# Order of gathered sums and dense multiplications on TensorE in a four-layer graph network

## What is computed

```python
h = jnp.maximum(_layernorm(x, axis=-1), 0.0)
neigh = jax.ops.segment_sum(h[src], dst, num_segments=N_NODES)
x = x + (jnp.maximum(((1.0 + eps[0]) * h + neigh) @ W1 + b1, 0.0) @ W2 + b2)
h = jnp.maximum(_layernorm(x, axis=-1), 0.0)
agg = jax.ops.segment_sum(h[src], dst, num_segments=N_NODES)
x = x + jax.nn.relu(agg / jnp.maximum(cnt, 1.0)[:, None] @ W_l.T + b_l + h @ W_r.T)
```

## Time and profile before

| | us |
|---|---|
| median of 3 runs (lowest, highest) | 6944.7 (6934.82, 6959.4) |
| profiled execution, its own time | 6939.28 |
| its span | 6937.5 |
| dense turns of layer 2 in the trace, about | 5258 to 5943 |
| dense turns of layer 3 in the trace, about | 6134 to 6846 |

### The profile page before, as it was taken

How to read it: one execution, slowest core, us unless ns; L and a number is a source line. 1 busy time by engine, 2 the same in 40 slices (tenths; PEclk the granted TensorE clock), 3 DMA queues, 4 the chain that set the end, 5 groups by cost and what they waited for, 6 DMA issues and landing times. The chain is left out here.

```text
span 6937.5 us, 158305 instructions
## 1 busy us (share of the span) xinstructions
PE 5351.4 (77%) x35997; PEld 4099.9 (59%) x35998; DVE 4547.1 (66%) x7277; ACT 2573.7 (37%) x6699; POOL 4647.9 (67%) x4837
## 2 busy tenths in 40 slices
PE   5788888888888775667777777777786999669996
PEld 5678877777877654445555555555563444435554
DVE  9888888888888755588888888888853111231112
ACT  5355555555555443235454444444440000110000
POOL 5377777777777622277777777777736777457776
PEclk6566566666666655578888888888888999789998
DMA  9221222222222266334444444444419999489996
GB/s 398 78 54 54 54 53 55 55 55 55 53 55 55 59 213 201 85 116 141 140 145 136 144 140 137 143 141 140 140 57 263 329 328 329 102 245 318 317 318 174
DMA packets 913080, 1053.41 MB, mean 152 GB/s; under 512 B 329373, under 2 KB 758063, under 8 KB 910720
## 3 DMA queue, kind: packets, MB, share of 16 engines
q10 hardware_dynamic: 460709, 626.59, 27.6%
q1 hardware_dynamic: 303644, 264.09, 13.4%
q0 software_dynamic: 148624, 161.51, 8.8%
HBM read 692.23 MB, written 359.54 MB: 152 GB/s over the span
## 5 line engine op out<-in xcount | busy, mean ns | idle before, releaser
L945 POOL DMA_INDIRECT sorted_tab<-msg,row_at x1661 | 1606.3, 967 | 653.0 <-issue 490.0
L1530 POOL DMA_INDIRECT a_rows<-a_tab,idx x1661 | 1567.8, 944 | 535.3 <-issue 507.5
L2090 POOL DMA_INDIRECT h_rows<-h_tab,idx x1216 | 1155.4, 950 | 532.9 <-issue 355.0
L1824 ACT ACTIVATE adj<-ps_adj 128x392 bf16<-128x392 f32 x2080 | 943.9, 494 | 1038.5 <-PE ps_adj L1755 1032.1
L835 PE MATMUL ps_at<-next_at,lo_t 128*128 128x98 f32 x3328 | 1046.5, 411 | 324.6 <-ACT next_at L898 253.4
L835 PEld LDWEIGHTS ps_at<-next_at,lo_t 128*128 128x128 f32 x3328 | 771.3, 286 | 375.3 <-issue 194.7
L1755 PE MATMUL ps_adj<-one_key,one_lo 128*128 128x392 bf16 x2080 | 683.2, 366 | 381.4 <-ACT adj L1824 361.4
L1640 DVE TENSOR_TENSOR one_key<-ps_iota,key_all 128x1960 bf16<-128x1960 f32 x416 | 911.5, 2191 | 0.0
L2289 PE MATMUL ps_dense<-pieces,x_nm 128*128 128x480 bf16 x3332 | 725.6, 368 | 192.9 <-DVE low L2173 114.3
L863 PE MATMUL ps_msg<-u_win,hot_t 128*128 128x64 f32 x3328 | 840.7, 349 | 5.5 <-DVE hot_t L768 5.3
L863 PEld LDWEIGHTS ps_msg<-u_win,hot_t 128*128 128x128 f32 x3328 | 778.5, 287 | 9.6 <-DVE hot_t L768 9.0
(11 more groups left out here) (297 smaller groups left out, 8816.6 us busy)
## 6 DMA issues: line engine op xcount, KB each, us to landing
pieces<-adj_tab ACTq DMA_DIRECT2D x204, 1440.0 KB
adj_tab<-adj ACTq DMA_DIRECT2D x208, 980.0 KB
pieces<-adj_tab ACTq DMA_DIRECT2D x68, 1560.0 KB
sorted_tab<-acc_t SPq DMA_DIRECT2D x16, 4030.0 KB
landed_rows<-sorted_tab SPq DMA_DIRECT2D x124, 520.0 KB
lo_row<-lo_tab SPq DMA_DIRECT2D x209, 256.0 KB
ends_of<-edge_t SPq DMA_DIRECT2D x208, 132.0 KB
sorted_tab<-msg,row_at POOLq DMA_INDIRECT x1661
```

The lines of the kernel that those rows point to most:

```text
L945: pool.indirect_dma_start(sorted_tab[:, :], bass.IndirectOffsetOnAxis(ap=row_at[:, r, k:k + 1], axis=0), msg[:, r, k, :], None).then_inc(s ...
L1530: pool.indirect_dma_start(dest[:, r, k, :], None, table[:, :], bass.IndirectOffsetOnAxis(ap=idx[:, r, k:k + 1], axis=0)).then_inc(landed[r ...
L1824: nc.scalar.activation(adj[:, b, :, k * WORD:(k + 1) * WORD], ps_adj[:, k % 2, 0:KEYS].rearrange("p (j d) -> p j d", d=WORD), ACT.Copy).th ...
L2090: pool.indirect_dma_start(rows_of[:, r, k, :], None, table[:, :], bass.IndirectOffsetOnAxis(ap=idx[:, r, k:k + 1], axis=0)).then_inc(lande ...
```

## The change

In the dense turns of both layers, PE does the products of step r first and the two pieces of step r second. `turn_own` and `own_terms` keep their places at the head of their steps. No other engine's program is changed.

```diff
                                 if layer == 3 and r == 3:
                                     own_terms(u)
+                                products(q, FIRST_A * RING + q, r, u, r % 2)
                                 for g, k in pieces_of(u, r):
                                     multiply(u, k)
-                                products(q, FIRST_A * RING + q, r, u, r % 2)
```

## The result

The changed kernel takes 7100.86 us (median of 3 runs, 7098.09 to 7107.81) against 6944.7: 156 us more by the medians. The ratio, estimated from all the runs, is 1.0232 with a 95% interval of 1.0214 to 1.0249. The forecast was 7078, range 7018 to 7115. Its profiled execution took 7098.09 us with a span of 7096.3.

A forecast was written before the change was run, and what follows sets the result against it. PE was taken to set the pace, with POOL and piece transfers close behind. The median 6944.7 plus 85 us for boundaries and layer starts and ends, plus 48 for clock falls, gave 7078 us; range 7018 to 7115.

The forecast's parts named there:

- What bounds the kernel: Dense turns of layers 2 and 3: PE sets the pace; in layer 2 POOL and piece transfers also need nearly 40 us.
- The boundary: Between turns PE waits 3.5 us for one-hots behind the block addition; with lost overlap +3.86, net +2.25 and +2.2 us.
- The turn without the clock: Dense turns if the granted clock stays at 1.00: 42.1 us in layer 2, 43.6 us in layer 3.
- The clock: At the 32 turn boundaries: PE's clock falls after some waits, 2.4 us each, 48 us in all; bounds 0 and 77.
- I take 20 falls: Clock falls expected at 20 of 32 boundaries, by position of the 3.5 us wait between 1.9 and 4.5 us.
- The row of 4.50: Profile row of layer 2's start: after 4.50 us of PE idle the granted clock was 0.50, from 5273 to 5278.
- the clock falls at every boundary: Rival for all 32 turn boundaries: a fall each, at 2.4 us or a little more, about 7107 us; chance 0.13.
- Start and end: Layer ends: first pieces lose their cover under DVE's clearing, 9 us per layer; layer 3's gathered tail shortens to 49 us.
- The transfers hid nothing in layer 2: Rival for layer 2: the 99.9% busy piece queue sets the pace and hides longer PE gaps, about 7020 us; chance 0.04.
- the boundary would be no wait: Rival at the turn's end: next one-hots are ready when piece 7 ends, saving 1.60 us per turn, 6909 us; chance 0.03.

The follow-up runs named there:

- the one-hots twice: Changed kernel, with DVE making the one-hots of each later turn's step 0 twice: 7150.7 us, ratio 1.0303 to the kernel before.
- the one-hots first: Changed kernel, with DVE making the next turn's step 0 one-hots before adding the finished block: 6929.95 us, ratio 0.9973 to the kernel before.
- the run with filler: Changed kernel plus 15 extra matmuls into an unused PSUM bank behind each turn's last piece: 7040.21 us, ratio 1.0140 to the kernel before.
- the run with less filler: Changed kernel plus 5 extra matmuls into an unused bank behind each turn's last piece: 7084.66 us, ratio 1.0210 to the kernel before.
- the run with the old first step: Changed kernel, but pieces before products in step 0 of turn 0 of each layer: 7092.43 us, ratio 1.0205 to the kernel before.

## Why the prediction was right, and where it was off

The measured 7100.86 us lies inside the wide range, but outside the band of the forecast itself, 7049 to 7097 for 8 to 28 falls. The direction and the mechanism of the wait were right; the range held because it took in a rival.

**What bounds the kernel** was read rightly. PE set the pace in both layers: when its turn grew, POOL (65.2 us of waiting) and the transfers (90.1%) followed, and when it shrank, the transfers stopped it in layer 2.

**The boundary** behaved as described, link by link: addition 0.25 us behind the last piece (0.27 foreseen), 2.76 us from its start to the end of the one-hots (2.70), 0.65 from there to the products (0.5 foreseen; the 0.65 of the earlier trace rows was the right one). The wait is 3.67 us instead of 3.5. The experiment with the one-hots twice shows that this chain sets the time, the one with the one-hots first that nothing else in the new order costs the turns anything.

**The turn without the clock** was mis-sized. With filler, so with the clock at 1.00, it is 42.63 us in layer 2 and 44.17 in layer 3; 42.1 and 43.6 were forecast. Of the half microsecond, 0.17 is the longer wait and 0.07 the gap before piece 0 (0.52 for 0.45); the rest is spread. Over 32 boundaries that is 17 us. Starts and clock-free turns together were put at 85 us; the run with filler is 95 over the median before.

**The clock** is the step that failed in both its factors. "I take 20 falls", interpolated between a wait of 1.90 us and one of 4.50, met 32; "2.4 us" a fall met 1.9. The price was taken from slow products and a slow first piece together, but in 10 boundaries of layer 2 the products were not slowed. The two errors partly cancel, which is luck: 48 us forecast, 61 measured. The sign given for 20 falls, a granted clock of about 0.95, could not tell them from 32: with 32 it is 0.95 and 0.94. The row of 4.50 was the nearer guide, and the run with less filler shows why the interpolation misled: at 2.6 us three boundaries in four already fall. The rival "the clock falls at every boundary" (7107) is what happened, with the smaller price. The Trainium skill ("TensorE: Matmul & The Clock Gate", section "HAM oscillation — how this bites in real kernels") had it so, that a recurring wait throttles PE in each iteration; the trace agrees, with 32 falls of 32, though not every turn starts cold, as the fast products in layer 2 show.

**Start and end.** 9 us per layer were forecast for the uncovered first pieces; the run with the old first step gets back 7.0 and 6.4, so this term was some 2 us a layer too large. The tail of layer 3, 49 us from the last piece to the last products, came out at 49.0 (7007.3 to 7056.3), with 4.30 us to the first products of the rest.

**The other rivals** fell. The transfers hid nothing in layer 2: their queue went down to 90.1%. That the boundary would be no wait needed the one-hots ahead of the addition; the run that makes them so is faster than before, at 6930, where the rival gave 6909. Most of the miss lies in layer 2, where the transfers hold it: its turn is 0.5 us shorter than before instead of 1.6.

**One expectation** went wrong in two experiments: POOL's 40.0 us a turn were to hold layer 2, but the versions that beat the kernel before do 39.3 to 39.4 there. POOL's gathers end some 26 us ahead of their products early in the layer (5317.0 for 5343.9 in the kernel before), and part of that lead is used up: with the one-hots first it is 25.7 us at the seventh step and 17.7 at the 67th.

## What to carry to other kernels

When work is reordered on the engine that sets the pace, look at the one place per iteration where a result of the whole iteration is handed over, and ask what still lies between that hand-over and its next use; three of four steps here had cover and the fourth lost it. A wait on TensorE has two prices, its length and what the clock takes afterwards, and the second (1.9 us a time) is seen only in the granted clock and in the longer matmuls that follow. The repair can lie on another engine: preparing the next step before finishing the last one made the same order on TensorE 0.3% faster than the original.

## What the runs showed that was not expected

Idle time does not have to be long for the clock to fall: at 1.90 us it fell at none of 32 boundaries, at 2.6 us at 24, at 3.67 us at all. The last two stand at the same place, between dense matmuls and products; the 1.90 us of the kernel before stand between products and dense matmuls, and whether the place matters was not tried. Useless matmuls in the wait pay for themselves: 15 of them per turn take 61 us off the changed kernel. And a turn in which PE is no longer late runs straight into the transfers: in layer 2 the kernel before, at 181.20 MB in 600 us, was within 1% of the 182.27 at which they hold it.
